# One core, eight layers in one kernel: order of products and scalings in the shared mixture, and one unread product in the last attention

## The reference

```python
# fourth block, "L1_ffn": eight experts and a shared one, two experts chosen per token
shared = silu(x @ sh_up_w + sh_up_b) @ sh_down_w + sh_down_b
scores = softmax(xf @ gate_w.T)
topk_w, topk_i = top_k(scores, 2)
topk_w = topk_w / (topk_w.sum(-1, keepdims=True) + 1e-20)
comb = (one_hot(topk_i, 8) * topk_w[..., None]).sum(axis=1)
h = silu(einsum('nd,edh->neh', xf, up_w) + up_b)
y = einsum('ned,ne->nd', einsum('neh,ehd->ned', h, down_w) + down_b, comb)
return y + shared
...
# seventh block, "L3_xattn": 16 heads of 8, softmax over 64 keys of the context
scores = einsum('bhqd,bhkd->bhqk', Q, K) / sqrt(8)
out = einsum('bhqk,bhkd->bhqd', softmax(scores), V) @ Wo.T + bo
```

## Time and profile before

| what | value |
|---|---|
| median of 3 runs | 1106.92 us (1106.59 to 1107.39) |
| the profiled execution's own time | 1109.05 us |
| its span, first to last instruction | 1107.0 us |
| mean granted TensorE clock | 0.981 of full speed |
| matmuls on PE, busy | 992.4 us (90%) |
| VectorE, ScalarE, GpSimd, busy | 786.3, 555.3, 236.5 us |

### The profile page before, as it was taken

The page is one execution under the profiler, slowest core; times in us unless marked ns, Lnnn a source line. Parts: engine busy times, 40 slices in busy tenths (PEclk is TensorE's granted clock), DMA queues, the critical chain, the costliest instruction groups (busy, mean ns, idle before and its releaser), DMA issues.

```text
span 1107.0 us, 33398 instructions
## 1 busy us (share of the span) xinstructions
PE 992.4 (90%) x12437; PEld 795.1 (72%) x12437; DVE 786.3 (71%) x1907; ACT 555.3 (50%) x1068; POOL 236.5 (21%) x247
## 2 busy tenths in 40 slices
PE   4789999989999997999989999888999988989887
PEld 4558888867777776777868778766778777656646
DVE  6776877587777776655496777566777667887877
ACT  2543443655555553434366565554656553445543
POOL 4651221122222221422010000000000002255300
PEclk9899999999999998999999999999999999999989
DMA  9300000000000000000000000000000000000001
GB/s 362 155 1 1 0 0 0 1 2 2 1 0 0 0 0 2 1 0 1 1 3 0 0 0 0 2 1 2 0 0 0 1 2 1 0 1 1 0 1 39
DMA packets 5926, 16.23 MB, mean 15 GB/s; under 512 B 729, under 2 KB 4962, under 8 KB 5218
## 3 DMA queue, kind: packets, MB, share of 16 engines
q1 hardware_dynamic: 5858, 15.29, 3.6%
HBM read 14.24 MB, written 1.05 MB: 14 GB/s over the span
## 4 chain that ended last, share of the span: by engine, by line
PE 61%; DVE 14%; issue 11%; DVEq 8%; ACT 3%; POOL 1%; POOLq 1%; ACTq 0%
PE banks L1852 9%; PE banks L1925 5%; PE banks L1897 5%; PE banks L1554 5%; PE banks L974 3%; PE banks L1885 3%; PE banks L1597 2%; PE banks L1913 2%; PE banks L1671 2%; PE banks L1469 2%; PE banks L1230 2%; PE banks L1637 2%; PE banks L1584 1%; PE banks L375 1%; PE banks L2387 1%
## 5 line engine op out<-in xcount | busy, mean ns | idle before, releaser
L1860 ACT ACTIVATE work<-banks 128x512 f32<-128x512 f32 x128 | 74.9, 600 | 70.8 <-PE banks L1852 70.8
L364 POOL TENSOR_TENSOR rstd<-var,nhalf 128x2 f32<-128x2 f32 x64 | 44.9, 702 | 297.1 <-DVE var L335 289.2
L1450 ACT ACTIVATE work<-work 128x1024 f32<-128x1024 f32 x64 | 67.9, 1060 | 43.3 <-DVEq L1446 25.8
L1852 PE MATMUL banks<-xT_all,weights 128*128 (+1 forms) x384 | 86.2, 380 | 2.3 <-ACT work L1974 1.6
L2008 DVE TENSOR_TENSOR work<-banks,neg_mask 128x512 f32<-128x512 f32 x64 | 40.9, 685 | 63.4 <-PE banks L1885 62.2
L1852 PEld LDWEIGHTS banks<-xT_all,weights 128*128 128x128 f32 x384 | 71.6, 190 | 13.7 <-ACT work L1974 2.4
L1012 ACT ACTIVATE work<-banks,weights 128x256 f32<-128x256 f32 x128 | 53.5, 472 | 54.6 <-PE banks L964 53.7
L1476 ACT ACTIVATE work<-banks 128x512 f32<-128x512 f32 x128 | 68.2, 604 | 12.0 <-PE banks L1469 7.7
L1925 PEld LDWEIGHTS banks<-weights,work 128*128 128x128 f32 x512 | 58.4, 191 | 15.0 <-ACT work L1974 15.0
L974 PE MATMUL banks<-weights,work 128*128 128x128 f32 x512 | 63.1, 276 | 5.4 <-DVE work L1121 5.0
L974 PEld LDWEIGHTS banks<-weights,work 128*128 128x128 f32 x512 | 60.9, 191 | 9.6 <-ACT work L1012 8.2
(11 more groups left out here) (349 smaller groups left out, 2291.5 us busy)
## 6 DMA issues: line engine op xcount, KB each, us to landing
weights<-wpack SPq DMA_DIRECT2D x1, 5381.5 KB, 32.2
weights<-wpack SPq DMA_DIRECT2D x1, 2060.0 KB, 12.6
weights<-wpack SPq DMA_DIRECT2D x1, 2049.0 KB, 16.9
weights<-wpack SPq DMA_DIRECT2D x1, 1160.5 KB, 19.2
x_all<-x_in SPq DMA_DIRECT2D x2, 512.0 KB, 4.7
ctxT_all<-ctxT_in SPq DMA_DIRECT2D x1, 1024.0 KB, 6.7
out<-x_all SPq DMA_DIRECT2D x8, 128.0 KB, 1.8
rows<-rows_in SPq DMA_DIRECT2D x1, 832.0 KB
```

Source lines behind the costliest of these rows:

```text
L1450: act.activation(sm[:, u, :], sm[:, u, :], ACT.Exp, scale=scale).then_inc(h["exp"].sem, 1)
L1852: ins = pe.matmul(bank(ring.bank(f"qk{c}"))[:, j * PT:(j + 1) * PT], wt[:, 2 * (c % 4) + j, :], cols(src, p), start=True, stop=True)
L1860: act.activation(dst.rearrange("p c t -> p (c t)"), bank(ring.bank(f"qk{c}")), ACT.Copy) \
```

## The change

Four edits. The router's drain goes from `route`; only the first pair's, in `tensor_head`, keeps it, and in the loop `inputs_used` is told by the first product of `up` 1 instead. `down` of pair p-1 moves ahead of the spreads of pair p. On VectorE `scale` moves from behind `sum_up` to the end of a part, behind `weigh` and `ending`, and `weigh` first waits until the coefficients of the pair before are transposed. In the first step of the last attention PE waits until bank 5 is emptied and writes one unread product of 512 columns there, ahead of the values.

```diff
--- before.py
+++ after.py
@@ -1198,13 +1198,13 @@
                     ins = pe.matmul(bk[:, 8 * u:8 * u + 8], xs[:, u * P:(u + 1) * P], w("m1_router"),
                                     start=True, stop=True)
                 ins.then_inc(banks_filled, 1)
-                pe.drain().then_inc(inputs_used, 1)
 
             def tensor_head(pe):
                 pe.wait_ge(weights_in[weight_group[s]], 16)
                 pe.wait_ge(act_emptied, s.pro.base["a"])
                 pe.wait_ge(dve_emptied, s.pro.base["v"])
                 route(pe, s.pro, 0, 0)
+                pe.drain().then_inc(inputs_used, 1)
 
             def tensor(pe, follow):
 
@@ -1222,13 +1222,15 @@
                                             start=False, stop=(e == 7))
                     ins.then_inc(y_filled, 1)
 
-                def up(ring, i, p, j):
+                def up(ring, i, p, j, read=None):
                     settle(pe)
                     pe.wait_ge(*ring.bank_free(i, f"up{j}"))
                     bk = bank(ring.bank(f"up{j}"))
                     for c in range(2 * j, min(2 * j + 2, 9)):
                         ins = pe.matmul(bk[:, (c % 2) * PT:(c % 2 + 1) * PT], upw[:, c, :], cols(xT_all, p),
                                         start=True, stop=True)
+                        if read and c == 2 * j:
+                            ins.then_inc(read, 1)
                     ins.then_inc(banks_filled, 1)
 
                 def part(ring, i, p, k, loop=False):
@@ -1236,7 +1238,7 @@
                     if ring is s.body:
                         settle(pe)
                         route(pe, ring, i, p + 1)
-                    up(ring, i, p, 1)
+                    up(ring, i, p, 1, inputs_used if ring is s.body else None)
                     up(ring, i, p, 2)
                     settle(pe)
                     pe.wait_ge(*comb_ready.at(p, 1))
@@ -1247,6 +1249,10 @@
                     ins.then_inc(banks_filled, 1)
                     up(ring, i, p, 3)
                     up(ring, i, p, 4)
+                    if loop:
+                        down(p - 1, 1 - k, ring.emptied_before(i, "b3"))
+                    elif p:
+                        down(p - 1, 1 - k, s.body.emptied(p - 1, "b3"))
                     pe.wait_ge(*ring.emptied(i, "combT"))
                     for g in range(4):
                         settle(pe)
@@ -1259,10 +1265,6 @@
                                             tile_position=(32 * g, 0))
                             if e:
                                 ins.then_inc(banks_filled, 1)
-                    if loop:
-                        down(p - 1, 1 - k, ring.emptied_before(i, "b3"))
-                    elif p:
-                        down(p - 1, 1 - k, s.body.emptied(p - 1, "b3"))
                     if loop or p > 1:
                         turn_normed(pe, g_of(s, p) - 1)
                     elif p == 0:
@@ -1362,11 +1364,12 @@
                         sort(ring, i, p + 1)
                     if late:
                         sum_up(p - 2)
-                    scale(ring, i, k)
                     if ring is s.body:
+                        v.wait_ge(banks_filled, ring.filled(i, "combT"))
                         weigh(p + 1)
                     if late:
                         ending(p - 2)
+                    scale(ring, i, k)
 
                 def head():
                     v.memset(small[:, 128:384], 0.0)
@@ -2456,6 +2459,9 @@
                 if turn:
                     settle(pe)
                     turn_normed(pe, g_of(s, p) - 1)
+                if ring is s.one:
+                    pe.wait_ge(*ring.emptied(i, "qk"))
+                    keep_busy(pe, 5, 1)
                 settle(pe)
                 values(ring, i, p)
                 settle(pe)
```

## The result

| | median, us | runs | against before, fast runs (95% interval) |
|---|---|---|---|
| before | 1106.59 | 15 | |
| changed | 1112.10 | 15 | 1.0048 (1.0032 to 1.0064) |
| changed, measured once more with the last experiments | 1111.12 | 10 | 1.0055 (1.0036 to 1.0074) |
| changed with two repairs (the last section of the experiments) | 1102.20 | 11 | 0.9964 (0.9947 to 0.9980) |

The change makes the kernel 0.5% slower, 5.5 us between the medians. Forecast was 1103.2, 3.7 us faster. The profiled execution of the changed kernel took 1112.61 us, with a span of 1110.8 us against 1107.0.

What follows compares the result with a forecast made beforehand. PE, busy 90% of the span, was taken to bound the kernel. Looped steps -6.0, last pair -0.45, entry +2.6, clock +1.7 and unread product -1.6 sum to -3.7: 1103.2 us from 1106.92, range 1101.0 to 1106.3.

Steps and rivals of the forecast that it cites:

- Is VectorE ready?: Looped steps: VectorE's stream add takes 5.7 us, PE reaches the down products after 6.2; margin half a microsecond.
- The clock behind the first stall: Behind pair 1's stall: half of 3.4 us at half clock, 1.7 us lost; bounds nothing and 5.0.
- the nearest row: Attention before the mixture: a PE idle of 3.32 us, then 0.7 us of work, then 3.4 us at half clock.
- a rival's term (3.4): One clock term is missed: first pair's stall costs 3.4 in place of 1.7, or product fails; 1104.9, chance 0.27.
- The first pair's stall: Router of pair 2 starts 3.35 us late, PE stands 3.2 us; 0.7 comes back, entry costs +2.6.
- Looped steps: Pairs 2 to 6: 1.2 us less a step, 6.0 in five; 11.3 from start to start, 12.47 before.
- The drain: Behind the router in looped steps: without it 0.28 us less a step, between nothing and 0.56.
- The rule of the Trainium skill: Router to next product: the whole hole of 0.39 would close, gaining another 0.5 us in five steps.
- The last pair: No router there; its wait of 0.28 before the spreads goes, with the overlap a gain of 0.45 us.
- The unread product: Last attention's first step: falls into idle ahead of the values, keeps the full clock, -1.6 us; bounds 0 and +0.4.
- The rivals: Forecast 0.45, one clock term missed 0.27, stall leaves clock alone 0.15, change doesn't hide what it says 0.08, slower 0.05.
- The rival on the slower side: First pair's stall brings 10 us of half clock, 5.0 lost; last attention's clock falls as before; 1108.1, chance 0.05.

Runs made afterwards that it cites:

- two repairs: Changed kernel; pair 0 scales ahead of weighing, and the last pair and next attention's queries wait for their own banks alone: 1102.20 us, 0.9964.
- Exact waits: Changed kernel; ahead of the last pair and the next attention's queries each product waits for its own bank, not all banks: 1105.60 us, 1.0006.
- VectorE's order alone: Kernel before, with scaling last on VectorE and nothing else; PE keeps spreads ahead of down products, and the drain: 1106.88 us, 1.0023.
- pair 0 as before: Changed kernel, but in pair 0 alone VectorE scales ahead of weighing: 1108.25 us, 1.0033.
- work in the stall: Changed kernel with three unread products of 512 columns ahead of the router of pair 2: 1104.74 us, 1.0001.

## Why the prediction was wrong, by its own steps

**The step that failed** is the one under "Is VectorE ready?". It followed the moved scaling into the next looped step, where its margins hold, and named the add for the down products as what is late next. It did not follow the scaling across the ends of the stage. There PE waits for the last of VectorE's counts, not for a bank, and the moved scaling is just that last count, with no down products behind the spreads to cover it. These two waits, 2.31 and 2.42 us, are 4.7 us that stand nowhere in the sum, nor among the rivals; with them the sum is +1.0 in place of -3.7. Exact waits gave 4.6 to 5.4 us back; with VectorE's order alone, where down products still stand behind the spreads, the last pair starts without a wait.

**The clock behind the first stall** was sized at 1.7 us, half of 3.4; it cost 3.1 (17.46 against 14.38 in pair 1, with the stall filled), because the half clock lasted from about 453.6 to 460.4, twice the stretch of the nearest row. That stood in the list as a rival's term (3.4), not in the sum: +1.4. The sum is then +2.4.

**The first pair's stall** was right in place and size: 3.11 us of wait for the first scaling where 3.2 was said.

**Looped steps** were right: 11.24 measured, 11.3 forecast; five steps gained 5.7, with 6.0 said. But sizes inside were off and cancelled, which is luck. The drain gave 0.54 a step in place of 0.28, close under the upper bound of 0.56: from router to next product there are 0.36 us (490.94 to 491.30), before 0.90 (497.72 to 498.62); alone it gave the same 0.54. Another 0.17 was not in the sum: transposes, first up products and router follow each other closer where the transposes don't wait (0.28 and 0.87 us from start to start, before 0.36 and 0.96). The rule of the Trainium skill, TensorE: Matmul & The Clock Gate, Step-by-step, that weight loads are pulled ahead of running products, was the better guess: the whole hole closes, and one step later the weight load of that product starts at 502.51, ahead of the router's end (502.17 + 0.51). Against this, the down products start 1.40 us after the last ups, not 1.3, the spreads 5.23 after the down products (494.73 to 499.96), not 5.04, and the transposes 1.07 after the spreads, not 0.94: 0.4 a step lost.

**The last pair** was said to gain 0.45 and lost 0.27, from the same sizes behind the ups (0.4 together) and from products that start after a wait, without the usual overlap (the ups 0.07, the queries 0.22).

**The unread product**: the mechanism holds. All nine profiles with the product (two of them of the changed kernel) have the full clock in that step, transposes 1.06 and scores 1.09; all four without it have half clock there, in three it covers the second transposes and the scores, or part of them. With VectorE's order alone it comes somewhat sooner, over values and transposes, and leaves the scores at 1.09. Like for like the step gains 1.6 us (15.84 to 14.22) and 1.5 (16.05 to 14.51), as forecast. The changed kernel takes 14.52 us (975.04 to 989.56), 1.3 less than before and not 1.6, since PE there waits 0.36 us for ScalarE ahead of the first transposes, a wait that the profile before doesn't have. As a gain in the median it did not show: 1.0004 with it alone, 0.9961 and 0.9964 without and with it. From the fourth scores to the end the traces take 121.2 to 124.5 us, with the product or without, and with half clock in different places of the stages behind, so that a gain of 1.6 is easily lost from sight. Whether it reaches the end in full is open.

**The rivals.** None of the five had the blanket waits. The rival on the slower side put its price on ten microseconds of half clock; the direction was right, but its mechanism was not the main one, and that half clock lasted 6.8 us.

With the waits (+4.7) and the clock (+1.4) the forecast's terms for the mixture alone sum to +4.0 us, against +5.3 in the trace. The last pair (0.7), the looped steps (0.3) and the rest of pair 1 (5.95 measured, 5.7 by the terms: 0.3) make up the difference. The medians differ by 5.5 us; with the 1.3 us that the last attention gains in the changed trace one would expect 4.0, which lies inside the interval (1.0032 to 1.0064).

What stays open is how often each wait meets half clock: of the eight waits of 2.3 and 2.4 us in the four profiles that have them (the changed kernel twice, pair 0 as before, work in the stall) three did. The repairs gave 1.7 to 2.4 us (pair 0), 4.6 to 5.4 (exact waits) and, together, 9; they need not add up, since each wait costs more or less by what the clock does behind it, and the intervals are near 2 us on either side. The filled stall's 5.2 to 6.0 us in the ratio, against 3.1 in its trace, is not explained either.

## What to carry to other kernels

When work is moved to the end of an engine's step, look up every wait on a *total* count of that engine, not on one buffer: at a change of loop or stage such a wait costs nothing as long as something else is last, and can cost nearly all of the moved work once it isn't (2.31 and 2.42 us of 2.48 here). And look at the first turn of a pipelined loop by itself; the cover that the steady turns have is missing there, and one exception for it (here four lines) can decide whether a change pays: exact waits alone came to 1.0006, with the exception to 0.9962.

## What the runs showed of the hardware that was not expected

- The same idle of 2.3 to 2.4 us of PE is followed by the full clock in one execution and by half clock in another: the same 12 and 32 products take 2.83 and 7.14 us in the changed kernel, 4.36 and 8.66 in the one with pair 0 as before, and the 32 take 10.16 in the changed kernel's second profile. The unfilled idle of 3.1 us was followed by half clock in all four profiles that have it.
- The half clock behind the 3.1 us lasted about 6.8 us (0.50 in 453.60 to 460.40), with PE busy for 6.44 of these.
- Much shorter idle was followed by half clock too: in all four profiles without the unread product, where PE waits 1.5 to 1.6 us ahead of the values and in three of them 0.64 us ahead of the next transposes. With the product, which leaves about 0.6 us of the first wait, none of nine shows it.
- Behind the last down products the spreads (32 rows) begin 2.21 us after these (497.75 to 499.96), the transposes (128 rows) 2.11 (529.70 to 531.81, before). Behind the spreads the bias product (9 rows) begins after 0.94 us, the transposes after 1.07.
